# Who sends the last regrouping, and where VectorE's small steps stand, in an attention and FFN kernel

## The chip, the cores and the metric

The kernel runs on one core of a Trainium2 chip. The metric is the device time of one execution in microseconds (us); before the change the median of three runs is 810.27 us (810.13 to 811.91).

## What is computed

The reference takes x of 16 batches, 512 tokens, 256 channels, all in float32. Cut to what matters:

```
xn  = layernorm(x)                        # mean and variance over 256 channels
qkv = xn @ w_qkv.T + b_qkv                # 16 heads of 16 channels
att = q @ k.T / 4 + bias(i - j)           # position bias per head, causal mask
out = softmax(att) @ v
x   = x + (out @ w_proj.T + b_proj)
        + fp8_quantised(xn) @ fp8_quantised(kernel) + bias   # bf16 result
```

## The kernel before

Each engine has its own program, written out by hand, and the engines meet at semaphores. The outer loop is over the batches: `body(b)` runs 16 times. Body 0, body 14 and body 15 are written out on their own; bodies 1 to 13 are a loop. A body has four units (g = 0 to 3, four heads each) of twelve slots (k = 0 to 11). A place in the program is written (g, k); slots of a body follow each other as (0, 0) to (3, 11).

In every slot TensorE (PE) makes one chunk of transposed scores for unit g of this body (`scores_T`, L640 and for units 0 and 1 also L643, into the three banks scoreT_a, b, c in turn) and one chunk of plain scores two units ahead (`scores`, L617, into score_a, b, c in turn). ScalarE (ACT) turns the transposed chunk into exponentials (L925). VectorE (DVE) takes the row maxima of the plain chunk (`chunk_max`, L1003). A bank is written again only when the chunk three slots earlier has been read: PE waits there for ACT, or for DVE. GpSimd (POOL) masks the diagonal blocks (L1201).

Between the slots stand other jobs, by tables of places at the head of the file. For PE: PV (probabilities times values, with denominators as an extra row, L666), MT (transposing the maxima, L601), QK and V and PJ (L550), FF (the quantised product, L593), T (transposing, L558). PV of unit 0, 1, 2 stands at (1, 0), (2, 3), (3, 3), and that of unit 3 at (0, 3) of the next body. QK, for the next batch, stands at (0, 6), (0, 9), (1, 6), (1, 9); both halves of FF stand at (2, 0). The second half of FF writes misc_b, the bank of the last QK, and so waits until DVE has read that: `QK_lo` (L991) at (1, 10), which itself follows ACT's read of the same bank (L832) at (1, 9). The other QK_lo steps are at (0, 7), (0, 10), (1, 7).

What the change touches:

- The regrouping. At k = 4 of each unit ACT copies the PV result of the unit before into OT (`out_T`, L898). Two DMAs then carry OT away (`send_attn`, L354 the attention rows, L355 the denominators). For units 0 to 2 SP issues them (`regroup`). For unit 3, at (0, 4) of the next body, ACT issues them itself, after waiting for its own L898 to have written.
- The inversion. DVE takes the reciprocal of the denominators (`invert`, L1010) once both of the last two denominator DMAs have landed. SP then stores the inverses to DRAM (L396) and loads them back spread over the channels (L408); POOL multiplies (`divide`, L1235) in unit 1, after its second mask.
- The layer norm statistics two batches ahead: four `stats` (L973) and one `aggregate` of four small instructions (L981).
- The quantiser pieces for the next batch: `quant_magic` (L1026 once, L1031 twice). ACT's `normalise`, from (3, 1) on, waits for them.

Within a slot DVE's order is chunk_max, T_lo, QK_lo, result, invert, stats, aggregate, quant_magic. SP's order at the start of a body is: `load_stack(b, 3)`, `load_max(b, 1)` (four DMAs, L341), `load_x(b + 2)`, `store_recips`, `spread_recips`, `load_stack(b + 1, 0)`, `load_max(b, 2)`, `regroup(b, 0)`.

Of the kernel before, what the change touches and what calls it, by code (L numbers as in the profile page):

```python
# [27 lines left out]
B, T, C = 16, 512, 256  # L28
# [44 lines left out]
XH_AT, FIRST_XH_AT = [(3, 9), (3, 10)], [(0, 2), (0, 2)]  # L73
XL_AT, FIRST_XL_AT = [(3, 10), (0, 0)], [(0, 3), (0, 3)]

INVERT_AT, LAST_INVERT_AT = (0, 6), (3, 8)
STATS_AT, AGGR_AT = [(1, 2), (1, 3), (1, 5), (1, 8)], (1, 9)
MAGIC_AT = [(2, 0), (2, 1), (2, 2)]


EARLY = 4
# [31 lines left out]
def due(jobs, g, k, lag=0):  # L113

    return [i for i, (jg, jk) in enumerate(jobs) if SLOTS * jg + jk == SLOTS * g + k - lag]
# [13 lines left out]
def build(nc, x, w_qkv, b_qkv, w_proj, b_proj, pos, ffn_w, s_in, s_k, ffn_b, feat_q, feat_k, out):  # L129
    with ExitStack() as ctx:  # L130
# [6 lines left out]
        def sem(name):  # L137
            return ctx.enter_context(nc.semaphore(name))
# [123 lines left out]
        ot_ready = sem("out_T_written")  # L262
# [54 lines left out]
        def misc_of(kind, i):  # L317

            return MBS[MISC_BANK[kind, i]]
# [19 lines left out]
        def send_max(eng, g):  # L339
            for h in range(HU):  # L340
                eng.dma_start(max_rows(g, h), MTS[2 * TT * h:2 * TT * h + 2 * TT, g % 2, :].bitcast(F32)) \  # L341
                    .then_inc(max_loaded[g], 16)

        def wait_alone(eng, always, *pairs):


            held = [(s, v if isinstance(v, int) else eng.compute_val(v)) for s, v in pairs]
            eng.wait_ge(*always)
            for s, v in held:
                eng.wait_ge(s, v)  # L350

        def send_attn(eng, b, g):
            r = 64 * (g % 2)
            eng.dma_start(attn_row(b)[r:r + HU * HD, g // 2, :], OT[0:P:2, :]).then_inc(ot_stored[g % 2], 16)  # L354
            eng.dma_start(DEN[32 * g:32 * g + 32, :], OT[1:P:2 * HD, :]).then_inc(den_loaded[g % 2], 16)  # L355
# [13 lines left out]
        def _(sp):  # L369
            def load_x(b):  # L370
                sp.dma_start(x_slot(b), x[bass.ds(b, 1), :, :].rearrange("o (t p) c -> p (o t) c", p=P)) \
                    .then_inc(x_loaded, 16)

            def load_stack(b, g):

                for u in (2 * g, 2 * g + 1):
                    sp.dma_start(STK[:, u, :, :].bitcast(F32), QKP[pair_rows(u), u // 4, :, :, :].bitcast(F32)) \
                        .then_inc(stack_loaded[g], 16)

            def load_max(b, g):  # L380
                sp.wait_ge(mts_ready, 4 * b + g + 1)
                send_max(sp, g)

            def regroup(b, g, early):

                if g == 0 and not early:

                    wait_alone(sp, (w_loaded, 16), (al_ready, b), (rc_ready, b), (ot_ready, 4 * b + g + 1))
                else:
                    sp.wait_ge(ot_ready, 4 * b + g + 1)  # L390
                send_attn(sp, b, g)

            def store_recips(b):

                wait_alone(sp, (w_loaded, 16), (rc_ready, b + 1), (rb_loaded, 32 * (b + 1)))
                sp.dma_start(recips.rearrange("h (e j) -> (h e) j", e=8), RDEN[:, :]).then_inc(rc_stored, 16)  # L396

            def spread_recips(b, last):

                if not last:  # L400

                    wait_alone(sp, (w_loaded, 16), (rc_stored, 16 * (b + 1)), (t_ready, 2 * (b + 3)))
                else:
                    sp.wait_ge(rc_stored, 16 * (b + 1))
                    sp.wait_ge(qm_done, 2 * B)
                for ct in range(CT):
                    src = recips[8 * ct:8 * ct + 8, :].unsqueeze(1).broadcast_to([8, HD, T])
                    sp.dma_start(RB[:, ct, :], src).then_inc(rb_loaded, 16)  # L408
# [58 lines left out]
            def store_out(b):  # L467
                sp.wait_ge(out_ready, 2 * (b + 1))
                sp.dma_start(out[bass.ds(b - 1, 1), :, :].rearrange("o (t p) c -> p (o t) c", p=P),
                             x_slot(b + 3)).then_inc(out_stored, 16)  # L470

            def body(b, first, last, load):
                if not first:
                    sp.wait_ge(st_ready, ROW * b)
                load_stack(b, 3)
                load_max(b, 1)
                if load:
                    if not first:
                        sp.wait_ge(out_stored, 16 * b)
                    sp.wait_ge(x_loaded, 16 * (b + 2))  # L480
                    load_x(b + 2)
                if not first:
                    store_recips(b - 1)
                    spread_recips(b - 1, last)

                if not last:
                    wait_alone(sp, (w_loaded, 16), (st_ready, ROW * b + SLOTS),
                               (ql_ready, 4 * (b + 1) + 2))
                    load_stack(b + 1, 0)
                load_max(b, 2)  # L490
                regroup(b, 0, first)

                if not last:
                    wait_alone(sp, (w_loaded, 16), (st_ready, ROW * b + 2 * SLOTS))
                    load_stack(b + 1, 1)
                load_max(b, 3)
                regroup(b, 1, first)

                if not last:
                    wait_alone(sp, (w_loaded, 16), (st_ready, ROW * b + 3 * SLOTS),  # L500
                               (ql_ready, 4 * (b + 1) + 4))
                    load_stack(b + 1, 2)
                if not last:
                    load_max(b + 1, 0)
                regroup(b, 2, first)
                if not first and not last:
                    store_out(b)

            body(0, True, False, True)
            with sp.Fori(1, B - 2) as b:  # L510
                body(b, False, False, True)
            body(B - 2, False, False, False)
            body(B - 1, False, True, False)
            store_recips_of(0, 12, B)
# [286 lines left out]
        def _(act):  # L801
# [88 lines left out]
            def out_T(b, g, skip_wait):  # L890

                act.wait_ge(pv_done, 4 * b + g + 1)
                if not skip_wait:

                    before = (g - 1) % 2, 16 * (2 * b + (g + 1) // 2)
                    act.wait_ge(ot_stored[before[0]], before[1])
                    act.wait_ge(den_loaded[before[0]], before[1])
                A(OT[:, :], misc_of("PV", g)[:, :], ACT.Copy).then_inc(ot_ready, 1)  # L898
                if g == 3:
                    act.wait_ge(ot_ready, 4 * b + 4)  # L900
                    send_attn(act, b, 3)

            def attn_hi(b, ct):
# [5 lines left out]
            def body(b, first, last, more):  # L909
                for g in range(G):  # L910
                    for k in range(SLOTS):
# [4 lines left out]
                        if k == OUT_AT and not (first and g == 0):  # L916
                            if not (last and g == 3):
                                max_T(*((b, g + 1) if g < 3 else (b + 1, 0)))
                            out_T(pb, pg, first and pg == 0)
# [37 lines left out]
            body(B - 2, False, False, False)  # L957
            body(B - 1, False, True, False)
            out_T(B - 1, 3, False)
            for ct in range(CT):  # L960
                act.wait_ge(div_done, B + ct)
# [5 lines left out]
        def _(dve):  # L967
# [51 lines left out]
            def quant_magic(b, part):  # L1019

                if part == 0:
                    if isinstance(b, int) and b < 2:
                        dve.wait_ge(qk_magic, b + 1)
                    else:
                        wait_alone(dve, (x_loaded, 16), (qk_magic, b + 1), (div_done, b - 1))
                    V.tensor_scalar(QE.bitcast(I32), QT.bitcast(I32), 0x7F800000, None, ALU.bitwise_and) \  # L1026
                        .then_inc(qe_done, 1)
                else:
                    dve.wait_ge(qe_done, b + 1)
                    ct = part - 1  # L1030
                    V.scalar_tensor_tensor(out=QM[:, ct], in0=QE[:, ct], scalar=E4_LEAST, in1=QM[:, ct],  # L1031
                                           op0=ALU.max, op1=ALU.mult).then_inc(qm_done, 1)
# [68 lines left out]
            def body(b, first, last, more):  # L1101
                for g in range(G):
                    nb, ng = (b, g + 2) if g < 2 else (b + 1, g - 2)
                    ahead = not (last and g >= 2)
                    for k in range(SLOTS):
# [25 lines left out]
                        if not last:  # L1131
                            for part in due(MAGIC_AT, g, k):
                                quant_magic(b + 1, part)
# [230 lines left out]
```

## Time and profile before

| | before |
|---|---|
| median of three runs | 810.27 us |
| the profiled execution, its time | 810.14 us |
| its span, first to last instruction | 808.4 us |
| PE busy / DVE / ACT / POOL | 752.4 / 624.6 / 578.6 / 531.1 us |
| mean granted clock of TensorE, as a share of full | 0.968 |

The span is split by engine into busy and idle time. Matmuls overlap in the pipeline, so the length of one is more than the time it takes from the next; where PE's speed is read, it is from the starts of its instructions.

### The profile page before, as it was taken

The numbers are of one execution on the slowest core, as the hardware profiler recorded it, in microseconds if no ns is written. First come the engines' busy times: TensorE is split into PE (matmuls) and PEld (weight loads), VectorE is DVE, ScalarE is ACT, GpSimd is POOL, SyncE is SP. The second block draws the span as 40 slices with busy tenths as digits, with TensorE's granted clock in tenths as the row PEclk, the third lists the DMA queues.
The fourth block names the chain that finished last, engine by engine and source line by source line (L and its number), as shares of the span: only waits on it lengthen the run. The fifth ranks groups of instructions, "written<-read, shape, count | busy, mean of one in ns | idle before, by whom it ended". The sixth has DMA issues, their size and how long they took to land.

```text
span 808.4 us, 23158 instructions
## 1 busy us (share of the span) xinstructions
PE 752.4 (93%) x6313; PEld 515.3 (64%) x6313; DVE 624.6 (77%) x2395; ACT 578.6 (72%) x1258; POOL 531.1 (66%) x525
## 2 busy tenths in 40 slices
PE   6889999999999999999999999999999999999883
PEld 3556566676666766666676667667676666667552
DVE  3869878887978888787887888798788878888612
ACT  3347868777877868777886777777787777777570
POOL 6435568676666767577666857666676767757570
PEclk8859999999999999999999999999999999999997
DMA  5603333534333253333434243443335334343202
GB/s 172 235 2 140 120 123 114 172 115 151 138 145 136 106 189 119 129 137 145 166 117 149 112 159 112 164 140 145 121 119 179 131 122 138 146 146 114 78 18 86
DMA packets 55612, 106.07 MB, mean 131 GB/s; under 512 B 10528, under 2 KB 30496, under 8 KB 55584
## 3 DMA queue, kind: packets, MB, share of 16 engines
q1 hardware_dynamic: 52680, 102.96, 36.2%
q10 hardware_dynamic: 2904, 2.77, 1.1%
q8 instruction: 13, 0.21, 0.1%
q14 instruction: 15, 0.12, 0.1%
HBM read 18.68 MB, written 8.91 MB: 34 GB/s over the span
## 4 chain that ended last, share of the span: by engine, by line
PE 69%; ACT 7%; DVE 7%; issue 6%; DMA 6%; SPq 3%; ACTq 1%; DVEq 1%; POOL 0%; POOLq 0%
PE misc_a L666 13%; PE misc_a L550 10%; PE misc_b L550 10%; PE scoreT_b L640 8%; PE scoreT_a L640 5%; PE score_a L617 4%; PE score_c L617 4%; DMA x_ring<-in_L_attn_x 4%; PE misc_b L666 3%; SPq L341 3%; ACT probs L925 3%; PE misc_b L601 2%; ACT xnT_hi L821 2%; PE scoreT_c L640 2%; DVE row_max L1003 1%
## 5 line engine op out<-in xcount | busy, mean ns | idle before, releaser
L1201 POOL TENSOR_SCALAR_AFFINE_SELECT probs<-probs 128x512 f32<-128x512 f32 x256 | 161.7, 642 | 231.1 <-ACT probs L925 229.5
L1003 DVE CUSTOM_DVE_ANT_0 score_b<-score_b,causal_mask_q 128x384 f32<-128x384 f32 (+3 forms) x321 | 162.0, 522 | 95.8 <-PE score_b L617 95.6
L1003 DVE CUSTOM_DVE_ANT_0 score_a<-score_a,causal_mask_q 128x512 f32<-128x512 f32 x319 | 174.9, 565 | 6.5 <-PE score_a L617 3.2
L925 ACT ACTIVATE probs<-scoreT_b 128x384 f32<-128x384 f32 (+1 forms) x256 | 134.4, 525 | 63.5 <-PE scoreT_b L640 21.1
L1003 DVE CUSTOM_DVE_ANT_0 score_c<-score_c,causal_mask_q 128x256 f32<-128x256 f32 (+3 forms) x384 | 172.0, 476 | 3.0 <-PE score_c L617 2.8
L925 ACT ACTIVATE probs<-scoreT_a 128x512 f32<-128x512 f32 (+1 forms) x256 | 145.4, 568 | 4.5 <-PE scoreT_a L643 3.7
L1003 DVE DVE_READ_ACCUMULATOR2_ANT row_max<- 128x1 f32 x1024 | 145.6, 142 | 0.0
L925 ACT ACTIVATE probs<-scoreT_c 128x384 f32<-128x384 f32 (+1 forms) x256 | 135.9, 531 | 3.4 <-PE scoreT_c L643 3.0
L666 PE MATMUL misc_a<-probs,v_ones 128*32 128x128 f32 (+3 forms) x1536 | 132.1, 440 | 0.4 <-POOL probs L1201 0.4
L640 PE MATMUL scoreT_b<-stacks 64*128 64x384 f32 (+3 forms) x320 | 120.0, 394 | 5.7 <-ACT probs L925 5.7
L617 PE MATMUL score_b<-stacks 64*128 64x384 f32 (+3 forms) x321 | 118.4, 401 | 1.4 <-DVE row_max L1003 1.4
L640 PE MATMUL scoreT_c<-stacks 64*128 64x256 f32 (+3 forms) x384 | 106.6, 309 | 8.9 <-ACT probs L925 8.9
L617 PE MATMUL score_a<-stacks 64*128 64x512 f32 x319 | 111.1, 380 | 2.7 <-DVE row_max L1003 2.6
L640 PE MATMUL scoreT_a<-stacks 64*128 64x512 f32 (+3 forms) x320 | 108.1, 358 | 5.0 <-DMA low_features<-neg_max_T 2.4
L640 PEld LDWEIGHTS scoreT_b<-stacks 64*128 64x128 f32 x320 | 57.0, 185 | 72.6 <-ACT probs L925 39.9
L617 PE MATMUL score_c<-stacks 64*128 64x256 f32 (+3 forms) x384 | 99.6, 313 | 0.5 <-DVE row_max L1003 0.2
L640 PEld LDWEIGHTS scoreT_c<-stacks 64*128 64x128 f32 x384 | 68.9, 187 | 15.9 <-ACT probs L925 14.0
L666 PEld LDWEIGHTS misc_a<-probs,v_ones 128*32 128x32 f32 x1536 | 59.7, 109 | 28.6 <-issue 12.3
L617 PEld LDWEIGHTS score_c<-stacks 64*128 64x128 f32 x384 | 65.8, 189 | 5.5 <-DVE row_max L1003 5.0
L617 PEld LDWEIGHTS score_a<-stacks 64*128 64x128 f32 x319 | 55.4, 188 | 20.4 <-DVE row_max L1003 16.9
L640 PEld LDWEIGHTS scoreT_a<-stacks 64*128 64x128 f32 x320 | 57.4, 187 | 12.0 <-issue 6.8
L898 ACT ACTIVATE out_T<-misc_a 128x512 f32<-128x512 f32 x48 | 28.7, 599 | 42.4 <-PE misc_a L666 42.4
(241 smaller groups left out, 1957.3 us busy)
## 6 DMA issues: line engine op xcount, KB each, us to landing
stacks<-qk_parts SPq DMA_DIRECT2D x128, 512.0 KB, 3.9
x_ring<-in_L_attn_x SPq DMA_DIRECT2D x16, 512.0 KB, 3.3
xn<-recips SPq DMA_DIRECT2D x31, 256.0 KB
out<-x_ring SPq DMA_DIRECT2D x15, 512.0 KB, 3.0
attn<-out_T SPq DMA_DIRECT2D x48, 128.0 KB, 2.6
stacks<-neg_max_T SPq DMA_DIRECT2D x128, 4.0 KB
attn<-out_T ACTq DMA_DIRECT2D x16, 128.0 KB, 2.7
low_features<-neg_max_T SPq DMA_DIRECT2D x124, 4.0 KB
```

The source lines that it names most:

```text
L341: eng.dma_start(max_rows(g, h), MTS[2 * TT * h:2 * TT * h + 2 * TT, g % 2, :].bitcast(F32)) \
L550: last = mm(o, l(ct), r(ct), start=(ct == 0 and i == 0), stop=(ct == CT - 1 and i == 2))
L601: last = mm(bank[0:HU * 2 * TT, 0:P], MX[:, g % 2, 32 * part:32 * part + 32], ident[:, :], start=(part == 0), stop=(part == 1))
L617: last = mm(SB_[n % 3][:, o:o + w], STK[rows, u, 0, P * qt:P * qt + P], STK[rows, u, 1, 0:w], start=True, stop=True)
L640: last = mm(bank, STK[rows, u, 1, P * j:P * j + P], STK[rows, u, 0, P * j:T], start=True, stop=(g >= 2))
L666: last = mm(bank[32 * i:32 * i + 32, P * j:T], VA[:, j, HU * g + i, :, :].rearrange("p d a -> p (d a)"), probs(g, j)[:, i, :], start=(j == ...
L821: A(XH[:, ct, :], misc_of("T", ct)[:, :], ACT.Copy).then_inc(xh_ready, 1)
L898: A(OT[:, :], misc_of("PV", g)[:, :], ACT.Copy).then_inc(ot_ready, 1)
L925: A(probs_slot(g, k), STB[(SLOTS * g + k) % 3][:, 0:w], ACT.Exp).then_inc(exp_done, 1)
L1003: last = V.tensor_tensor_reduce(bank, bank, CMQ[:, T - w:T], 1.0, LEAST, ALU.add, ALU.max, MX[:, g % 2, 8 * h + 4 + qt:8 * h + 5 + qt])
L1201: last = GP.affine_select(out=d, in_=d, compare_op=ALU.is_ge, fill=0.0, base=0, pattern=[[0, HU], [1, P]], channel_multiplier=-1)
```

## The change

Three edits. SP issues the two regrouping DMAs of unit 3, after the maxima of unit 1 and ahead of the load of x; only in the last body does ACT still issue those of its own unit 3, at the end. The inversion of the loop moves from (0, 6) to (0, 8); the last one, `LAST_INVERT_AT`, stays. The statistics and the quantiser pieces take other slots.

```diff
-INVERT_AT, LAST_INVERT_AT = (0, 6), (3, 8)
-STATS_AT, AGGR_AT = [(1, 2), (1, 3), (1, 5), (1, 8)], (1, 9)
-MAGIC_AT = [(2, 0), (2, 1), (2, 2)]
+INVERT_AT, LAST_INVERT_AT = (0, 8), (3, 8)
+STATS_AT, AGGR_AT = [(1, 3), (1, 3), (1, 6), (1, 6)], (1, 7)
+MAGIC_AT = [(2, 3), (2, 6), (2, 9)]
@@ SP, body @@
                 load_stack(b, 3)
                 load_max(b, 1)
+                if not first:
+                    regroup(b - 1, 3, False)
                 if load:
@@ ACT, out_T @@
                 A(OT[:, :], misc_of("PV", g)[:, :], ACT.Copy).then_inc(ot_ready, 1)
-                if g == 3:
-                    act.wait_ge(ot_ready, 4 * b + 4)
+                if g == 3 and isinstance(b, int) and b == B - 1:
+                    act.wait_ge(ot_ready, 4 * B)
                     send_attn(act, b, 3)
```

## Rows read from the trace of the kernel before

**Rows 1.** The page, part 1: busy time, share of the span, instructions of each engine.

```profile
PE 752.4 (93%) x6313; PEld 515.3 (64%) x6313; DVE 624.6 (77%) x2395; ACT 578.6 (72%) x1258; POOL 531.1 (66%) x525
```

**Rows 2.** The waits of the whole span: engine, line, waited for: us in total, times, longest.

```profile
DVE denominators_inv L1010 <- DMA denominators<-out_T: 26.4, 15, 2.0
...
ACT probs L925 <- issue: 19.0, 13, 1.6
```

**Rows 3.** The tile of denominators: its reciprocals, min/median/max ns, first and last start.

```profile
L1010 DVE RECIPROCAL denominators_inv<-denominators x15: 552/553/555, 107.4 to 755.1; 128x64 f32<-128x64 f32 x15
```

**Rows 4.** Timeline of PE, body 8, unit 0: start, length, line, tiles, [idle before].

```profile
427.63 0.44 PE L640 MATMUL scoreT_b<-stacks 64*128 64x384 f32 x1
...
430.52 0.44 PE L640 MATMUL scoreT_b<-stacks 64*128 64x384 f32 x1 [0.15 <-ACT probs L925]
...
435.04 1.07 PE L666 MATMUL misc_a<-probs,v_ones 128*32 128x512 f32 x8
```

**Rows 5.** Timeline of PE, the same slots of unit 1, and FF behind them.

```profile
439.49 0.44 PE L640 MATMUL scoreT_b<-stacks 64*128 64x384 f32 x1
...
442.16 0.44 PE L640 MATMUL scoreT_b<-stacks 64*128 64x384 f32 x1
...
443.34 0.51 PE L550 MATMUL misc_b<-xnT_hi,w_qkvT_hi 128*128 128x512 f32 x1
...
446.21 0.61 PE L593 MATMUL misc_a<-ffn_w_q,xq 128*128 128x256 bf16 x4
...
447.26 0.61 PE L593 MATMUL misc_b<-ffn_w_q,xq 128*128 128x256 bf16 x4 [0.44 <-DVE qk_parts L991]
```

**Rows 6.** Timeline of ACT and its queue, the same body.

```profile
427.94 0.60 ACT L898 ACTIVATE out_T<-misc_a 128x512 f32<-128x512 f32 x1 [1.22 <-PE misc_a L666]
...
429.30 0.56 ACTq L355 DMA_DIRECT2D denominators<-out_T  x1
...
429.98 0.49 ACT L925 ACTIVATE probs<-scoreT_b 128x384 f32<-128x384 f32 x1 [1.45 <-issue]
...
445.05 1.12 ACT L832 ACTIVATE qk_parts<-misc_b,b_qkv 128x1024 fp32r<-128x1024 f32 x1 [0.53 <-PE misc_b L550]
```

**Rows 7.** Timeline of DVE, the same body, units 0, 1 and 2.

```profile
431.60 0.55 DVE L1010 RECIPROCAL denominators_inv<-denominators 128x64 f32<-128x64 f32 x1 [1.72 <-DMA denominators<-out_T]
...
442.75 0.57 DVE L1003 CUSTOM_DVE_ANT_0 score_b<-score_b,causal_mask_q 128x384 f32<-128x384 f32 x1 [0.72 <-PE score_b L617]
...
444.68 0.42 DVE L973 BATCH_NORM_STATS2 bn_six<-x_ring 128x6 f32 x1
...
446.46 0.75 DVE L991 SCALAR_TENSOR_TENSOR qk_parts<-misc_b,b_qkv,qk_parts 128x512 fp32r<-128x512 f32 x1
...
454.88 0.57 DVE L1003 CUSTOM_DVE_ANT_0 score_b<-score_b,causal_mask_q 128x384 f32<-128x384 f32 x1 [0.91 <-PE score_b L617]
...
457.29 0.43 DVE L1003 CUSTOM_DVE_ANT_0 score_b<-score_b,causal_mask_q 128x256 f32<-128x256 f32 x1 [0.52 <-PE score_b L617]
```

**Rows 8.** Timeline of SP's queue and of POOL, the same body.

```profile
426.74 2.72 SPq L341 DMA_DIRECT2D low_features<-neg_max_T  x4
...
444.50 2.38 POOL L1235 TENSOR_TENSOR attn<-attn,xn 128x1024 f32 x1
```

**Rows 9.** Timeline of PE in body 14, units 0 and 1.

```profile
705.58 0.44 PE L640 MATMUL scoreT_b<-stacks 64*128 64x384 f32 x1
...
712.96 1.07 PE L666 MATMUL misc_a<-probs,v_ones 128*32 128x512 f32 x8
...
721.22 0.50 PE L550 MATMUL misc_b<-xnT_hi,w_qkvT_hi 128*128 128x512 f32 x1
...
724.88 0.61 PE L593 MATMUL misc_b<-ffn_w_q,xq 128*128 128x256 bf16 x4 [0.33 <-DVE qk_parts L991]
```

**Rows 10.** Timeline of PE in body 15, the last, unit 0.

```profile
753.52 0.44 PE L640 MATMUL scoreT_b<-stacks 64*128 64x384 f32 x1 [1.52 <-ACT probs L925]
...
756.25 0.38 PE L617 MATMUL score_b<-stacks 64*128 64x256 f32 x1 [1.14 <-DVE row_max L1003]
```

## The prediction

> **What bounds the kernel now.** I read the page, then the waits of the whole span, then one body engine by engine. PE is busy 93% of the span [rows 1], so it is the engine to follow; its losses are short. The waits show two stalls that come once a body: DVE waits 26.4 us in 15 times for the denominators, and ACT stands idle 19.0 us in 13 times after issuing [rows 2]. The reciprocals start from 107.4 to 755.1 us in 15 steps [rows 3], so a body takes (755.1 - 107.4) / 14 = 46.3 us and a slot 0.96 us.
>
> Neither stall matters unless PE feels it. The kernel has its own control for that: PE does nearly the same work in slots 4 to 12 of unit 0 and of unit 1 (three pairs of scores, a QK, three pairs, a QK, three pairs; the last pair of unit 0 has one matmul more). In unit 0 these take from 427.63 to 435.04, 7.41 us [rows 4]. In unit 1 they take from 439.49 to 446.21, 6.72 us [rows 5]. Unit 0 loses 0.69 us a body; for the extra matmul, which runs beside its neighbour, I take off 0.08, an estimate between 0 (wholly beside it) and 0.2 (half of its length of some 0.44, the other half overlapping the next). That leaves 0.61. Of it 0.22 falls before the pair of slot 7 (430.52 - 427.63 = 2.89 against 442.16 - 439.49 = 2.67), which waits for an exponential of ACT [rows 4, 5], and the rest behind it, where DVE has restarted only at 431.60 [rows 7].
>
> The second loss is in FF: its second half starts at 447.26, with PE idle 0.44 [rows 5], because QK_lo runs on DVE only at 446.46 [rows 7].
>
> **One rule changes how these are summed.** The idle column gives PE 0.15 us before slot 7 and 0.44 before the second FF [rows 4, 5], and starts give more. The Trainium skill (Perfetto Trace Analysis, Identifying the Most-Contended Engine) says that matmul busy time is a poor measure of distance to the limit, since matmuls are pipelined. By the idle column alone the change could give back little over 0.15 + (0.44 - 0.33) = 0.26 us a body (0.33: what stays in body 14, below) and the time would be about 806.5. I count by starts.
>
> **The change, part by part.**
>
> *ACT no longer issues.* Its L898 ends at 428.54; the second issue ends at 429.86 and the next exponential starts at 429.98, 1.45 us late [rows 6]. All of it goes, in bodies 1 to 15. Alone it is worth little: in body 14, where PE's pair of slot 7 is not late, the stretch from 705.58 to 712.96 still takes 7.38 us [rows 9], because DVE is then the next to be late. The two edits must be priced together.
>
> *SP issues instead.* SP issues four maxima DMAs from 426.74 for 2.72 us, to 429.46 [rows 8]; OT is ready before that. So the wait that is added costs nothing: the issue of the rows starts at about 429.6, and that of the denominators, each taking about 0.6, at about 430.2, 0.9 us later than the 429.30 of before [rows 6]. Landing took 431.60 - 429.30 = 2.30 us from the issue [rows 6, 7], so they land at about 432.5. Behind these two on SP stand the load of x, the store and the spread of the inverses, two stack loads and the next maxima: all move by about 1.2 us at most, until the stack loads, which waited for the end of unit 0 anyway. Readers of x are DVE's statistics at (1, 3), some eleven slots on.
>
> *The inversion two slots on.* DVE idles 1.72 us before L1010 at 431.60 [rows 7]. When does it get to the new place? In unit 1 the first instruction behind the chunk of slot 8 is L973 at 444.68 [rows 7], 5.19 us behind the start of the stretch. The same in unit 0 is 427.63 + 5.19 = 432.8, later than 432.5. The stall goes to 0, with 0.3 us to spare. The reciprocal's own half microsecond stands then where unit 1 has a statistic and the aggregate, which is no less, so the control holds for it. Its result comes about 1.3 us later than before (432.8 against 431.60). The product that needs it starts on POOL at 444.50 [rows 8], 12.9 us behind the old reciprocal; two transfers of 2.3 and their issues lie between, so it is hidden. If that cover were gone, the bill would be up to 1.3 us a body.
>
> *Worth of the two together.* 0.61 in each of bodies 1 to 13, and in body 14, by its own rows and the same control of 6.7 to 6.8, 0.6 to 0.7. 14 x 0.61 = 8.6 us. Bounds: 0.22 if DVE stays late (14 x 0.22 = 3.1), 0.69 if the extra matmul costs nothing (9.7). In the last body PE has no QK to hide behind: it idles 1.52 and then 1.14 us in slots 7 and 10 [rows 10]. The first wait goes but for a tenth or two. The second mostly stays, in slot 8's place: a QK fills over half of the 2.67 us ahead of slot 7, so without it DVE reaches (0, 8) over a microsecond sooner, and the denominators land no sooner. Between 0 and 2.66, I take 1.0.
>
> *Statistics.* The same four L973 and four L981 stay; what counts is how much stands between DVE's idle time at 442.03 to 442.75 (0.72) and QK_lo at 446.46 [rows 7]. One statistic leaves this stretch and the aggregate stays in it, at (1, 7). Body 14 has no statistics at all: from the QK at 721.22 to the second FF at 724.88 it takes 3.66 us [rows 9], against 447.26 - 443.34 = 3.92 [rows 5]. The gain is at most 0.26, for then ACT's read of the same bank is what ends last: L832 starts at 445.05 and takes 1.12 [rows 6], to 446.17, 0.29 before QK_lo. The statistic that leaves has a length of 0.42 [rows 7], so I take the full 0.26 in bodies 0 to 13: 3.6 us. Lower bound 0. The two statistics at (1, 6) stand in that idle time, lengthened by the one that leaves (1, 5); the two at (1, 3) where DVE is no longer behind.
>
> *Quantiser pieces.* I put each at 0.65 us of DVE, an estimate between the 0.42 of L973 and the 0.75 of L991 [rows 7]. At (2, 6) there are 0.91 us idle before the chunk that follows, at (2, 9) 0.52 [rows 7], and at (2, 3) what the three pieces free ahead of it, 1.95. Only the third sticks out, by 0.1, and two further score banks are between that and PE. I take 0. ACT's normalise stands four slots behind the last piece. Before, they delayed nothing on PE either: behind FF the chain hangs on QK_lo. Bounds: -0.1 to +0.1 a body.
>
> **Sum.** 8.6 + 1.0 + 3.6 = 13.2. From the profiled execution's 810.14, of which 808.4 is span and 1.7 lies around it, this gives 796.9; the median of the runs shown is 0.13 higher. **I forecast 797.0 us.**
>
> **Rivals.**
>
> *SP is the slower path.* The denominators land a microsecond later than I reckon, and DVE waits again, at (0, 8). For it: SP's queue is the fuller one, with 2.72 us of issues just ahead [rows 8]. The Trainium skill (Perfetto Trace Analysis, DMA Optimizations) says that where descriptor generation limits, DMAs should be balanced over the issuing engines, which speaks against moving ACT's share to SP. Landing at 433.5 instead of 432.5 lets DVE off 0.7 late; PE's next need of it is at (1, 0), about 0.2 further, so some 0.5 of the 0.61 is lost: 14 x 0.5 = 7. Time about 804. Against: SP is idle between 429.46 and its next task. Chance 0.15.
>
> *Only unit 0 gains.* The aggregate kept ahead of QK_lo eats the statistic that left. 810.14 - 9.6 = 800.5. Chance 0.12.
>
> *The gain is absorbed*, by a stretch in which ACT sets the pace: 810. Against: ACT waits for PE, 1.22 and 0.53 us, in the same body [rows 6]. Chance 0.05.
>
> *Slower.* The quantiser pieces find no room: DVE takes 0.65 us before the chunk of (2, 4), (2, 7) and (2, 10), and PE waits for the bank. Three in full cost 3 x 0.65 x 15 = 29, time 826; it decides from about 0.9 us a body, that is one and a half pieces uncovered. At two, 810.14 + 19.5 - 13.2 = 816. For: the idle 0.52 at (2, 9) is shorter than a piece. Against: a gap of 0.91 and a ring of three banks [rows 7]. Chance 0.04.
>
> The change does what it says; no part is dead.
>
> **How the numbers follow.** Forecast 0.64, with its own range 794 to 799.5 (control 0.69 instead of 0.61, last body 0 to 2.66; the mean granted clock of 0.968 has falls in it, and one may come sooner or later). The rivals at 800.5 and 804 extend the range: 793.5 to 804.0. Faster by over 0.2% (1.6 us): 0.64 + 0.15 + 0.12 and a little of the absorbed case, 0.92; within 0.2%, what a measurement here can't tell from none: 0.04; slower 0.04.
>
> **What would show it.** In the changed trace: no idle time of ACT after L898 in unit 0; L354 and L355 on SP's queue right behind four L341; L1010 one to two us later against PE, with idle under 0.3; unit 0's stretch 6.8 us, like unit 1's; the second FF 3.66 behind its QK; a body of 45.4 us. I am wrong if L1010 still waits over 0.5, if unit 0's stretch stays over 7.1, or if PE waits for DVE behind (2, 3), (2, 6) or (2, 9).

## The result, and the profile after

The changed kernel takes 818.62 us, median of 4 runs (817.50 to 820.13), beside 811.09 us for the kernel before (4 runs, 810.13 to 812.26): a ratio of 1.0093, with a 95% interval of 1.0069 to 1.0118. The forecast was 797.0. The profiled execution took 820.13 us with a span of 818.4, 10.0 more than before's, at a mean granted clock of 0.960.

In the changed kernel every line past 476 stands two lower down: L1031 is now L1033, L1012 is the inversion. From the page of the changed kernel, part 1, beside [rows 1]: PE and DVE are busier by 12 and 27 us with the same instructions, so instructions got longer.

```profile
PE 764.3 (93%) x6313; PEld 520.1 (64%) x6313; DVE 651.6 (80%) x2395; ACT 581.3 (71%) x1258; POOL 526.5 (64%) x525
```

The waits of DVE in the changed kernel, and the tile of denominators, beside [rows 2, 3]: the wait for the denominators has gone from 26.4 us in 15 times to 1.4 in one, and ACT's row of 19.0 us after issuing is no longer in its waits. But the reciprocals run from 110.7 to 764.4, so a body takes 46.7 us in the mean, not 45.4.

```profile
DVE denominators_inv L1012 <- DMA denominators<-out_T: 1.4, 1, 1.4
```

```profile
L1012 DVE RECIPROCAL denominators_inv<-denominators x15: 547/548/553, 110.7 to 764.4; 128x64 f32<-128x64 f32 x15
```

The timelines of SP's queue and of ACT in body 8 of the changed kernel, beside [rows 6, 8]. SP issues rows and denominators right behind its four maxima. Body 8 starts at 429.87 here and at 421.96 before, so the denominators are issued 8.53 us into the body, 1.19 later than ACT's issue of before (429.30 - 421.96 = 7.34). ACT goes from L900 into the next exponential without idle time.

```profile
434.64 2.72 SPq L341 DMA_DIRECT2D low_features<-neg_max_T  x4
437.77 0.59 SPq L354 DMA_DIRECT2D attn<-out_T  x1
438.40 0.61 SPq L355 DMA_DIRECT2D denominators<-out_T  x1
...
446.12 3.78 SPq L341 DMA_DIRECT2D stacks<-neg_max_T  x4
```

```profile
435.85 0.60 ACT L900 ACTIVATE out_T<-misc_a 128x512 f32<-128x512 f32 x1 [1.23 <-PE misc_a L668]
436.34 0.48 ACT L927 ACTIVATE probs<-scoreT_b 128x384 f32<-128x384 f32 x1
```

PE in the same body, beside [rows 4, 5]. Unit 0's stretch, from 435.54 to 442.52, takes 6.98 us instead of 7.41; the second FF starts 454.54 - 450.82 = 3.72 behind its QK instead of 3.92. So far the change gives what it should, if less of it. The last four rows are the pairs at (3, 1), (3, 2) and (3, 3) and the PV behind the last of them: they stand 0.63, 0.62 and 0.74 apart.

```profile
435.54 0.44 PE L642 MATMUL scoreT_b<-stacks 64*128 64x384 f32 x1
...
441.74 0.44 PE L642 MATMUL scoreT_a<-stacks 64*128 64x512 f32 x1
...
442.52 1.06 PE L668 MATMUL misc_a<-probs,v_ones 128*32 128x512 f32 x8
...
450.82 0.51 PE L552 MATMUL misc_b<-xnT_hi,w_qkvT_hi 128*128 128x512 f32 x1
...
454.54 0.61 PE L595 MATMUL misc_b<-ffn_w_q,xq 128*128 128x256 bf16 x4 [0.20 <-DVE qk_parts L993]
...
466.46 0.49 PE L642 MATMUL scoreT_b<-stacks 64*128 64x512 f32 x1
...
467.09 0.39 PE L642 MATMUL scoreT_c<-stacks 64*128 64x512 f32 x1
...
467.71 0.39 PE L642 MATMUL scoreT_a<-stacks 64*128 64x512 f32 x1
...
468.45 1.06 PE L668 MATMUL misc_b<-probs,v_ones 128*32 128x512 f32 x8
```

The same four in the kernel before, PE in body 8: 0.34, 0.23 and 0.32 apart. From the pair at (3, 1) to PV the changed kernel takes 1.99 us instead of 0.89. PE regains 0.35 behind PV: from there to the pair at (3, 4) it takes 2.71 (468.45 to 471.16) instead of 3.06 (460.07 to 463.13). Some 0.75 is lost.

```profile
459.18 0.49 PE L640 MATMUL scoreT_b<-stacks 64*128 64x512 f32 x1
...
459.52 0.39 PE L640 MATMUL scoreT_c<-stacks 64*128 64x512 f32 x1
...
459.75 0.39 PE L640 MATMUL scoreT_a<-stacks 64*128 64x512 f32 x1
...
460.07 1.06 PE L666 MATMUL misc_b<-probs,v_ones 128*32 128x512 f32 x8
```

DVE and then POOL in body 8 of the changed kernel, ahead of that. The quantiser piece L1033 at (2, 6) takes 0.97 us and the one at (2, 9) 2.14, and the chunk of (2, 10) waits behind it until 465.97.

```profile
461.11 0.97 DVE L1033 SCALAR_TENSOR_TENSOR quant_work<-xn,quant_work 128x512 f32<-128x512 f32 x1
...
463.90 2.14 DVE L1033 SCALAR_TENSOR_TENSOR quant_work<-xn,quant_work 128x512 f32<-128x512 f32 x1
465.97 0.42 DVE L1005 CUSTOM_DVE_ANT_0 score_b<-score_b,causal_mask_q 128x256 f32<-128x256 f32 x1
```

```profile
459.14 2.39 POOL L1242 TENSOR_TENSOR attn_lo<-attn,attn_hi 128x1024 fp32r<-128x1024 f32 x1
462.76 0.63 POOL L1203 TENSOR_SCALAR_AFFINE_SELECT probs<-probs 128x512 f32<-128x512 f32 x1 [1.23 <-ACT probs L927]
463.37 2.13 POOL L1209 TENSOR_TENSOR xnT_bf<-xnT_bf,b_ffn 128x1024 bf16<-128x1024 bf16 x1
465.55 1.59 POOL L1203 TENSOR_SCALAR_AFFINE_SELECT probs<-probs 128x512 f32<-128x512 f32 x2
```

This is how it reaches PE. DVE has read the bank of (2, 10) only at 466.69, and PE's plain scores of (3, 1), which go into that bank, start at 466.75 (the row below, PE in the changed kernel). That is 0.29 behind their partner at 466.46; before, the two started 0.01 apart (459.18 and 459.19). The next two banks follow in the same way, at 467.38 and 468.03.

```profile
466.75 0.49 PE L619 MATMUL score_b<-stacks 64*128 64x512 f32 x1
```

Read the ends, not the starts. POOL's L1242 ends at 459.14 + 2.39 = 461.53, and the second piece ends at 462.08, 0.55 later. L1209 ends at 465.50, and the third piece at 466.04, 0.54 later. A piece that starts beside one of these POOL instructions ends as if it had begun to work only when POOL was done.

The same line over the whole span, in the changed kernel and then in the kernel before (min/median/max ns): with the place the length grows to half as much again and to three times, for data of the same size. Before the change one piece of 32 was long too, 1.14 us in body 0; it is taken up in the last section.

```profile
L1033 DVE SCALAR_TENSOR_TENSOR quant_work<-xn,quant_work x32: 683/1070/2161, 42.3 to 742.2; 128x512 f32<-128x512 f32 x32
```

```profile
L1031 DVE SCALAR_TENSOR_TENSOR quant_work<-xn,quant_work x32: 681/691/1140, 42.2 to 728.4; 128x512 f32<-128x512 f32 x32
```

**The bill.** I took the time from pair to pair of PE in bodies 3 to 12 of both traces, the median of each slot. A body gets shorter by 0.42 us in unit 0 and 0.21 at FF, together 0.62; then slots (3, 1), (3, 2) and (3, 3) add 0.29, 0.40 and 0.07. Net +0.14. From start to start, bodies 2 to 13 add 2.1 us together, body 14 0.2, body 0 2.1, body 1 4.3 and the last with its end 1.2: the 10.0 of the span.

The two dear bodies pay for more than that. In body 1 it is something else: PE waits for the maxima of unit 2 at (2, 0), and behind that wait the granted clock is 0.50 from 124.8 to 131.6 us, the lower of its two levels, 1.2 GHz. The second fence has the windows around it (us, busy times, granted clock, DMA share, GB/s).

```profile
124.88 0.79 PE L642 MATMUL scoreT_a<-stacks 64*128 64x512 f32 x1 [1.70 <-DMA stacks<-neg_max_T]
```

```profile
118.00:124.00 6.00, 5.18 (x39) 3.86 (x39) 5.54 (x27) 4.73 (x10) 2.40 (x3) 1.00 0.80 235
124.00:132.00 8.00, 7.12 (x35) 3.62 (x39) 4.34 (x14) 4.84 (x10) 3.99 (x8) 0.57 0.36 136
132.00:138.00 6.00, 5.85 (x64) 4.74 (x56) 3.81 (x16) 3.76 (x9) 3.56 (x4) 1.00 0.08 26
```

In body 0 the held piece costs 1.38 us at (3, 1), and the granted clock is 0.50 from 90.7 to 94.1, in slot (3, 3), which takes 1.69 longer. The kernel before has neither of these two stretches. The second experiment, which moves only the pieces, has the one of body 0 again, from 91.3 to 94.7. That the waits caused the falls of the clock is still inferred from their order.

### The profile page after: what moved, and what is told of

It reads as the page before. It is cut to its first block, busy times and chain, and to the rows that moved or that the text cites. A ratio compares the mean times of both kernels' runs of the same rounds, so it can differ in the third digit from the quotient of the medians.

```text
span 818.4 us, 23171 instructions
## 1 busy us (share of the span) xinstructions
PE 764.3 (93%) x6313; PEld 520.1 (64%) x6313; DVE 651.6 (80%) x2395; ACT 581.3 (71%) x1258; POOL 526.5 (64%) x525
## 4 chain that ended last, share of the span: by engine, by line
PE 71%; ACT 8%; DMA 6%; issue 5%; DVE 5%; SPq 4%; POOL 0%; ACTq 0%; DVEq 0%; POOLq 0%
PE misc_a L668 12%; PE misc_a L552 11%; PE misc_b L552 9%; PE scoreT_b L642 8%; PE scoreT_a L642 5%; PE misc_b L668 5%; PE score_c L619 4%; DMA stacks<-neg_max_T 4%; PE score_a L619 4%; SPq L341 3%; ACT probs L927 3%; PE scoreT_c L642 2%; PE misc_b L603 2%; PE scoreT_b L645 1%; ACT xnT_hi L823 1%
## 5 line engine op out<-in xcount | busy, mean ns | idle before, releaser
L1203 POOL TENSOR_SCALAR_AFFINE_SELECT probs<-probs 128x512 f32<-128x512 f32 x256 | 165.5, 657 | 244.4 <-ACT probs L927 242.7
L642 PE MATMUL scoreT_c<-stacks 64*128 64x256 f32 (+3 forms) x384 | 104.7, 305 | 9.0 <-ACT probs L927 9.0
L900 ACT ACTIVATE out_T<-misc_a 128x512 f32<-128x512 f32 x48 | 28.7, 598 | 43.5 <-PE misc_a L668 43.1
```

The costliest lines, as they stand in the source:

```text
L642: last = mm(bank, STK[rows, u, 1, P * j:P * j + P], STK[rows, u, 0, P * j:T], start=True, stop=(g >= 2))
L1203: last = GP.affine_select(out=d, in_=d, compare_op=ALU.is_ge, fill=0.0, base=0, pattern=[[0, HU], [1, P]], channel_multiplier=-1)
```

## The experiments

The theory: a piece is held while POOL reads SBUF, and that, at (2, 9) above all, turns a gain of some 0.63 us a body into a loss. The rivals: there is simply no room in those slots (the rival named beforehand), or the new sender is at fault. The ratio is to the kernel before on the same chip, with its 95% interval. "A body" is the sum of the slot medians, as above.

**The changed kernel with the pieces back in their old slots.**

```diff
-MAGIC_AT = [(2, 3), (2, 6), (2, 9)]
+MAGIC_AT = [(2, 0), (2, 1), (2, 2)]
```

> The changed kernel with the quantiser pieces back at (2, 0), (2, 1), (2, 2). Theory (port): the changed kernel loses its time because the quantiser piece at (2, 9) runs on DVE while POOL runs its bias addition, and is held until POOL is done (2.14 us against 0.69). Then all 32 pieces take 0.69 again, unit 3 loses nothing, a body of the loop is 0.62 us shorter than before the change (46.32 to 45.70), and the time is about 801 to 805, what is open being how much the first two bodies still lose. Rival (SP path): the loss comes from the maxima that SP sends later, behind the moved regrouping. Then the time stays at 812 or more, and PE still waits at (2, 0).

Measured: 801.84 us (799.10 to 803.82), ratio 0.9883 (0.9856 to 0.9911); a body of 45.67, 0.64 less than before. In this kernel's trace the pieces have their old length:

```profile
L1033 DVE SCALAR_TENSOR_TENSOR quant_work<-xn,quant_work x32: 679/684/1094, 43.6 to 720.5; 128x512 f32<-128x512 f32 x32
```

The pieces are the loss; the rest of the change is a gain. This version beats both kernels. It has neither of the two stretches at the lower clock, and bodies 0 and 1 are each shorter in it than before the change.

**The kernel before with only the pieces moved.**

```diff
-MAGIC_AT = [(2, 0), (2, 1), (2, 2)]
+MAGIC_AT = [(2, 3), (2, 6), (2, 9)]
```

> The kernel before with only the quantiser pieces moved to (2, 3), (2, 6), (2, 9). Port: the third piece takes about 2.1 us, slots (3, 1) to (3, 3) of PE lose 0.76 us a body, 15 x 0.76 = 11, so about 822, a little more with the first bodies. SP path: SP's queue is untouched, so no loss: 811.

Measured: 825.04 us (822.88 to 827.68), ratio 1.0164 (1.0136 to 1.0192). A body is 0.77 us longer, all of it at (3, 1) to (3, 3), as in the changed kernel; in this trace:

```profile
L1031 DVE SCALAR_TENSOR_TENSOR quant_work<-xn,quant_work x32: 682/994/2157, 42.2 to 746.5; 128x512 f32<-128x512 f32 x32
```

The cost doesn't need the new sender or the new statistics.

**The changed kernel with POOL's bias addition one mask later.** DVE's program is untouched, so the slots hold what they held; only POOL's partner moves.

```diff
                     mask(b, g, 1)
-                    if g == 2:
-                        ffn_bias(b)
                     if g == 1 and not first:
                         divide(b - 1)
                     mask(b, g, 2)
+                    if g == 2:
+                        ffn_bias(b)
```

> The changed kernel, with POOL's bias addition (L1209) moved behind its last mask of unit 2, so that it doesn't run beside the piece at (2, 9); DVE's program is untouched. Port: the third piece falls from 2.14 to about 0.7 us and the time to that of the run with the pieces put back, 801 to 805. Rival (slots too full): what costs is that a piece stands at (2, 9) at all, with 0.52 us of room; then DVE's lateness stays and the time with it, about 818.

Measured: 802.18 us (798.38 to 804.31), ratio 0.9887 (0.9861 to 0.9913); a body of 45.67. DVE and then POOL of this kernel in body 8:

```profile
449.97 0.69 DVE L1033 SCALAR_TENSOR_TENSOR quant_work<-xn,quant_work 128x512 f32<-128x512 f32 x1
...
453.21 0.70 DVE L1005 CUSTOM_DVE_ANT_0 score_b<-score_b,causal_mask_q 128x512 f32<-128x512 f32 x1 [0.55 <-PE score_b L619]
453.82 0.69 DVE L1018 TENSOR_TENSOR x_ring<-misc_a,x_ring 128x512 f32 x1
```

```profile
451.61 1.23 POOL L1203 TENSOR_SCALAR_AFFINE_SELECT probs<-probs 128x512 f32<-128x512 f32 x2 [2.15 <-ACT probs L927]
452.82 2.14 POOL L1209 TENSOR_TENSOR xnT_bf<-xnT_bf,b_ffn 128x1024 bf16<-128x1024 bf16 x1
```

The third piece stands in the same slot and takes 0.69 us; the whole 0.77 is gone, though the second piece, still beside L1242, takes 0.99 in body 8 (447.17). So the slots have room, and the rival of no room falls. It also shows who is held: L1209 now runs beside chunk maxima and `result` (453.82), which read PSUM and one tile of SBUF, and these keep their length.

The Trainium skill (SBUF — State Buffer, Who interferes with whom) states this as a rule: VectorE and GpSimd share one pair of SBUF ports, taken for a whole instruction, and a VectorE instruction with two SBUF inputs, or in a mode that uses both ports, can't run beside a GpSimd instruction that reads SBUF; one with at most one SBUF input, outside those modes, isn't touched. These traces agree, with 2.14 against 0.69 us and with the 0.69 of L1018. I read the new places of the pieces for their room [rows 7] and not for who runs beside them.

**The changed kernel with other slots for the pieces:** the first piece, which reads one SBUF tile (L1028), beside L1242, and the third just behind L1209.

```diff
-MAGIC_AT = [(2, 3), (2, 6), (2, 9)]
+MAGIC_AT = [(2, 4), (2, 9), (2, 10)]
```

> The changed kernel with the quantiser pieces at (2, 4), (2, 9), (2, 10). The first piece (L1028, 1024 columns, one input from SBUF) then stands beside POOL's L1242, which reads two inputs from SBUF until some 1.5 us later; the second (two inputs) beside the bias addition. If only DVE operations with two SBUF inputs are held, as the chunk maxima (PSUM and SBUF) suggest, L1028 keeps its 0.69 us. If it is any operation that reads and writes SBUF alone, it takes 2.0 to 2.2. In both cases the second piece takes about 2.1 and the third, at (2, 10), meets POOL's L1222 or holds it up. Time: 820 or more, as two or three collisions stand in unit 2 instead of one and a half.

Measured: 824.05 us (822.73 to 826.94), ratio 1.0172 (1.0142 to 1.0202). The line of the first piece over the whole span of this kernel, then its DVE and its POOL in body 8:

```profile
L1028 DVE TENSOR_SCALAR xn<-quant_work x16: 685/2010/2097, 41.8 to 742.1; 128x1024 int32<-128x1024 int32 x16
```

```profile
460.21 2.01 DVE L1028 TENSOR_SCALAR xn<-quant_work 128x1024 int32<-128x1024 int32 x1
...
464.92 1.28 DVE L1033 SCALAR_TENSOR_TENSOR quant_work<-xn,quant_work 128x512 f32<-128x512 f32 x1
...
466.71 0.68 DVE L1033 SCALAR_TENSOR_TENSOR quant_work<-xn,quant_work 128x512 f32<-128x512 f32 x1
```

```profile
459.29 2.38 POOL L1242 TENSOR_TENSOR attn_lo<-attn,attn_hi 128x1024 fp32r<-128x1024 f32 x1
...
463.51 2.14 POOL L1209 TENSOR_TENSOR xnT_bf<-xnT_bf,b_ffn 128x1024 bf16<-128x1024 bf16 x1
```

Here it was decided that one SBUF input doesn't save an instruction: L1028 takes 2.01 instead of 0.69. It does 1024 columns in the 0.69 in which L1033 does 512, twice the rate; the two-port modes in the Trainium skill's rule would be that. A wider rule, that any instruction from SBUF to SBUF is held, doesn't fit [rows 7, 8]: L973 has one SBUF input and writes to SBUF, stands at 444.68 inside POOL's L1235 (444.50 to 446.88), and takes 0.42, its median length over the span. The ends again: 459.29 + 2.38 = 461.67, L1028 ends at 462.22, 0.55 later; L1209 ends at 465.65, the second piece at 466.20, 0.55 later. The second piece was not held for its expected 2.1 us but for 0.6, since L1028's delay had pushed it into the tail of L1209. The third piece did not meet L1222, as was expected; it meets two masks. PE loses 0.96 at (2, 8) and 0.28 at (2, 9).

**The kernel before with the first two edits** (SP as sender, the inversion at (0, 8)), statistics and pieces as they were.

```diff
-INVERT_AT, LAST_INVERT_AT = (0, 6), (3, 8)
+INVERT_AT, LAST_INVERT_AT = (0, 8), (3, 8)
@@ SP, body @@
                 load_max(b, 1)
+                if not first:
+                    regroup(b - 1, 3, False)
@@ ACT, behind L898 @@
-                if g == 3:
-                    act.wait_ge(ot_ready, 4 * b + 4)
+                if g == 3 and isinstance(b, int) and b == B - 1:
+                    act.wait_ge(ot_ready, 4 * B)
                     send_attn(act, b, 3)
```

> The kernel before with only SP sending the last regrouping and the inversion at (0, 8); statistics and quantiser pieces as before. Both theories of unit 0: 0.42 us a body less, as in the changed trace, 14 x 0.42 + 1 = 7: about 804. FF's second half then still comes late by 0.4. If the SP path costs in the first bodies (PE waiting at (2, 0) of body 1 for maxima), up to 2 to 4 us of it are given back: 806 to 808.

Measured: 805.16 us (801.52 to 806.97), ratio 0.9920 (0.9892 to 0.9949); a body is 0.42 shorter, all in unit 0.

**Each of the two alone.** First the inversion at (0, 8) with ACT as sender:

```diff
-INVERT_AT, LAST_INVERT_AT = (0, 6), (3, 8)
+INVERT_AT, LAST_INVERT_AT = (0, 8), (3, 8)
```

> The kernel before with only the inversion at (0, 8); ACT still sends. DVE's wait of 1.7 us at slot 6 goes, ACT's 1.45 stays. If the two stalls cover each other, as body 14 suggested (one of them gone, nothing gained), a body is 0.0 to 0.1 us shorter: 810 to 811. If they add up, DVE's share of the 0.42 is gained: 0.2 a body, 808.

Measured: 813.36 us (12 runs, 812.01 to 817.48), ratio 1.0028 (1.0012 to 1.0044). Both expectations, no change and a gain, missed by 2 us or more. A body is 0.13 longer, with the loss at (1, 0). DVE no longer waits for the denominators, but ACT keeps its stall, as its waits in this kernel say:

```profile
ACT probs L925 <- issue: 19.0, 13, 1.6
```

Then SP as sender, with ACT's edit as in the version of both, and the inversion at (0, 6):

```diff
 INVERT_AT, LAST_INVERT_AT = (0, 6), (3, 8)
@@ SP, body @@
+                if not first:
+                    regroup(b - 1, 3, False)
```

> The kernel before with only SP sending the last regrouping; the inversion stays at (0, 6). ACT's stall goes, but the denominators land 0.9 us later and DVE waits about 2.6 us instead of 1.7 at slot 6. Then PE's waits for DVE at (0, 11) to (1, 1) grow by more than ACT's share is worth: +0.3 to +0.6 us a body, 815 to 820. If ACT's stall were what bounds unit 0, it would be -0.2 a body instead, 808.

Measured: 832.26 us (831.81 to 832.90), ratio 1.0261 (1.0237 to 1.0284). Worse than either side of the change and worse than expected. DVE's waits in this kernel:

```profile
DVE denominators_inv L1012 <- DMA denominators<-out_T: 42.3, 15, 2.9
```

DVE waits 2.8 us each time against 1.8 before [rows 2]. PE loses 0.75 and 0.80 at (0, 10) and (0, 11), against the 0.38 that ACT gives before that: a body is 1.18 longer. That the rings of banks are used up by then is my reading; no run varied them. Part of the 832 is the clock: in the profiled execution it is at 0.50 for 3.4 us in each of bodies 1, 7 and 11, and these lose 1.1 to 1.6 more than the other bodies of the loop. +0.13 and +1.18 alone, -0.42 together: the two edits are one.

**The 801.84 us version with SP's stack load ahead of the spread of the inverses.** In the changed kernel unit 0 of the next stack lands late. SP has two issues more ahead of it, its four maxima take 3.78 us to issue where they took 2.76, and PE waits for them at (2, 0) in 5 bodies (4.0 us in all, against 0.8 in one).

```diff
                 if not first:
                     store_recips(b - 1)
-                    spread_recips(b - 1, last)
                 if not last:
                     ...
                     load_stack(b + 1, 0)
+                if not first:
+                    spread_recips(b - 1, last)
                 load_max(b, 2)
```

> Run 1 (pieces put back) with SP loading the next stack before it spreads the inverses. Theory: in the changed kernel and in run 1, PE waits now and then at (2, 0) because the stack load goes out 0.8 us later than before, lands 1.5 us later, and the maxima behind it just miss PE. With the stack first, its landing goes back to before's 20.5 us from the body's start, the waits at (2, 0) vanish (in body 1 and body 8 of run 1, 0.5 to 1 us), and the time is 1 to 2 us under run 1: about 800. Rival: the spread is then the one that is late, POOL's product in unit 1 waits, or the load takes as long as ever: 802 or more.

Measured: 804.24 us (802.75 to 806.06), ratio 0.9921 (0.9899 to 0.9943), against 0.9883 without it. About 800 was expected; 802 or more was what the rival gave, and its mechanism is in the trace. The second stack load of body 8 lands 18.3 us into the body instead of 23.1, and the waits at (2, 0) shrink from 2.0 to 1.2 us. But (2, 6) takes 0.18 more in the median body. The two intervals overlap, so the times alone don't show the cost; the medians of the slots do.

The 0.18 is the hold again, this time at an old slot. POOL's product of unit 1 now waits for its transfers, 5.6 us in 11 times where the 801.84 us version has 0.6 in one, so its masks come later and one of them meets the first piece at (2, 0), which takes 0.90 us in the median instead of 0.69. POOL, DVE and PE of this version in body 8:

```profile
442.73 1.23 POOL L1204 TENSOR_SCALAR_AFFINE_SELECT probs<-probs 128x512 f32<-128x512 f32 x2
```

```profile
443.34 1.16 DVE L1029 TENSOR_SCALAR xn<-quant_work 128x1024 int32<-128x1024 int32 x1
```

```profile
447.65 0.44 PE L620 MATMUL score_a<-stacks 64*128 64x384 f32 x1 [0.19 <-DVE row_max L1006]
```

The masks end at 443.96 and the piece at 444.50, 0.54 later. PE then waits for a bank of DVE's, six slots on. The bodies bear it out: in 4 to 6 and 8 to 13 L1029 takes 0.88 to 1.16 us, and they are 0.29 to 0.55 shorter than before the change; in 1 to 3 and 7 it takes 0.68 to 0.73, and they are 0.60 to 0.78 shorter. So a piece can be held by a late POOL even where nobody moved it.

**The 801.84 us version with the second half of FF a slot later.**

```diff
-FF_AT = [(2, 0), (2, 0)]
+FF_AT = [(2, 0), (2, 1)]
```

> Run 1 (pieces put back) with the second half of FF one slot on, at (2, 1), so that QK_lo has a pair of scores more of time before PE needs its bank. In run 1 PE still waits there for about 0.2 us a body. If that wait goes and ACT, which reads the second half at (2, 1), isn't held, a body is 0.2 us shorter: 14 x 0.2 = 3, so about 799. If ACT's read of FF then comes late and holds up the exponentials, it is the same or slower, 802 to 804.

Measured: 805.08 us (803.64 to 808.02), ratio 0.9914 (0.9892 to 0.9936). A body stays at 45.67; the slots from (1, 11) to (2, 3) share the time differently, and their sum is the same. A miss: FF's idle time is no loss that moving the second half recovers. The intervals of this and the unmoved version overlap, so a cost isn't shown either.

## Why the prediction was wrong

**The step that failed** is "Quantiser pieces": "I put each at 0.65 us of DVE ... I take 0. Bounds -0.1 to +0.1 a body." Their length was right where they stood before, and three slots have room for 0.65. It is wrong for these places: the second takes 0.97 and the third 2.14, because POOL's L1242 and L1209 run there. They cost PE 0.77 us a body, 11.6 us over 15 bodies by that median, and 13.8 alone as timed (825.04 - 811.28). In the profiled execution of that run body 0, with 2.6, has more than its share, and so has the last body, with 3.2, though it has no piece; the falls of its clock stand elsewhere than before. The 0.52 of idle time that I read at (2, 9) [rows 7] was right; what I left unread is POOL's timeline in that window. In the kernel before it has this row, over the whole of the idle time ahead of 457.29:

```profile
456.09 2.15 POOL L1207 TENSOR_TENSOR xnT_bf<-xnT_bf,b_ffn 128x1024 bf16<-128x1024 bf16 x1
```

The rival on the slower side had the place and gave 816 to 826, at 0.04; but its mechanism was lack of room, and moving POOL's instruction alone undid it. "PE waits for DVE behind (2, 9)" was named as what would prove me wrong, and did.

**The two edits priced together** was right in kind, as the three runs with them show (-0.42, +0.13, +1.18). The size was 0.61, and came out at 0.42. My control took off 0.08 for the extra matmul of the last pair. In the changed kernel the two stretches are equal up to that pair: 435.54 to 441.74 is 6.20, and so are unit 1's, 446.97 to 453.17. The pair itself, up to PV, takes 442.52 - 441.74 = 0.78, and unit 1's, up to FF, 453.73 - 453.17 = 0.56; before they took 0.79 and 0.52. So the extra matmul, together with whatever PV and FF differ in, costs 0.22 to 0.27, more than my upper bound of 0.2. With 0.27 the control would have given 0.69 - 0.27 = 0.42, as measured; the term is 14 x 0.19 = 2.7 us too large.

**The denominators** went as forecast: issued 1.19 instead of 0.9 later, and the reciprocal 10.99 us into the body instead of 9.64, 1.35 later against 1.3. DVE doesn't wait. The rival of SP as the slower path fell for this wait, but its sense came back elsewhere: with the inversion unmoved it costs 1.18, and SP's fuller queue makes the maxima of unit 2 late.

**"Behind these two on SP ... all move by about 1.2 us at most"** was too low and missed the landing. In body 8 the load of x is issued 9.63 us into the body instead of 8.08, the first spread 13.29 instead of 11.79, 1.5 later each; the first stack load of the next body 14.86 instead of 13.92. I named only the statistics as readers. The stacks and maxima at (2, 0) are readers too, and in body 1 PE waits 1.70 us there.

**Statistics and FF:** 0.21 instead of 0.26 a body. QK_lo starts at 453.74 with ACT's read of the bank ending at 452.53 + 1.11 = 453.64, so DVE is still 0.10 behind ACT.

**The last body** was to give 1.0. With its end it costs 1.2 us in the changed kernel and gives 1.7 in the 801.84 us version, whose half-clock stretches lie elsewhere; the term can't be told from the clock.

With the pieces where they were, the same sum would have been 14 x 0.42 + 14 x 0.21 = 8.8 plus the last body; 9.4 was measured (811.28 to 801.84). The rest of the forecast stands, 4 us short of its size.

## What to carry to other kernels

Before an instruction of VectorE is moved, lay its new window over GpSimd's timeline, not only over VectorE's idle time: in these runs an instruction whose operands were both in SBUF, or that ran at twice the rate, and that started beside a large GpSimd instruction or beside a mask, ended half a microsecond after GpSimd's, however much room its slot had. Compare the ends of the two; equal offsets give a hold away. And before an edit that delays GpSimd, do the same the other way round: its late instructions can meet VectorE's where nothing was moved. Two edits at the two ends of one transfer should be priced and tried as one: here each alone was a loss.

## What the runs showed of the hardware

- A held VectorE instruction ends 0.54 to 0.55 us after the GpSimd instruction it stands beside, in all four cases read (466.04 after 465.50, 462.08 after 461.53, 462.22 after 461.67, 466.20 after 465.65). Over all the bodies of the changed kernel and of the experiments in which pieces stand beside L1242 or L1209 it is 0.54 to 0.56. Only its own last half microsecond is left by then.
- The hold works the other way too, when VectorE starts first. In the changed kernel two masks behind the held piece take 1.59 us (465.55) where the two of the third experiment take 1.23. In the kernel before, L1168 (128x4), 0.02 us behind DVE's L1026 of 448.36, takes 0.73 and ends at 449.11, 0.06 after it; in the changed kernel, where no piece stands there, the same instruction takes 0.20.
- A mask, 0.64 us long, is enough to hold a piece. The kernel before shows it once, in body 0: the third piece takes 1.14, and ends at 81.51, 0.54 after the mask's 80.97. These are its DVE and POOL:

```profile
80.37 1.14 DVE L1031 SCALAR_TENSOR_TENSOR quant_work<-xn,quant_work 128x512 f32<-128x512 f32 x1
```

```profile
80.33 0.64 POOL L1201 TENSOR_SCALAR_AFFINE_SELECT probs<-probs 128x512 f32<-128x512 f32 x1
```

- One small GpSimd instruction did not hold. In the kernel before, L1170 (128x4) runs from 449.19 to 450.21, and the piece started at 449.57 beside it takes its 0.69 us, by the rows below, POOL and then DVE of the kernel before. By the rule of the Trainium skill cited above, a full block, it would have taken over a microsecond; the measurement decides. L1168 of the same size was itself held, so size alone is not the reason, and what sets L1170 apart stays open.

```profile
448.38 0.73 POOL L1168 TENSOR_SCALAR var_eps<-mean_var 128x4 f32<-128x4 f32 x1
449.19 1.02 POOL L1170 TENSOR_TENSOR rstd<-var_eps,neg_half 128x4 f32<-128x4 f32 x1
```

```profile
449.57 0.69 DVE L1031 SCALAR_TENSOR_TENSOR quant_work<-xn,quant_work 128x512 f32<-128x512 f32 x1
```

- In body 8, four maxima of 4 KB behind two stack loads of 512 KB take SP 3.78 us to issue when they follow at once (changed kernel), and 2.76 when they follow 1.6 us later (before). What slows the issue was not tried.
